# An xLSTM cell, attention and a mixture of experts on one core: x1 read in place, the experts' stages a slot further apart, the last stage in the experts' program

## The reference, cut to what matters

```
x  (32, 256, 128)                                  # B, T, D
# part 1: a gated recurrence over T, in every one of the 128 channels
pre = layernorm(x) @ W + b ;  i, f, o, z = split(pre)
m_t = max(f_t + m, i_t);  c = f_s*c + i_s*tanh(z);  n = f_s*n + i_s;  h = sig(o)*c/(n+eps)
x1 = x + h / rms(h) * scale
# part 2: on layernorm(x1)
q, k, v = split(layernorm(x1) @ w_qkv)             # 16 heads of 8
o = softmax(causal(q k^T / sqrt(8))) v @ w_o
h = layernorm(layernorm(x1) + o, g1, b1)
probs = softmax(h @ wg); the two best of 8 experts, weights normalised
moe = sum over the two of  w_e * (gelu(h @ w1_e + bb1_e) @ w2_e + bb2_e)
out = x1 + layernorm(h + moe, g2, b2)
```

## Time and profile before

| | us |
|---|---|
| median of 3 runs | 1063.59 (1061.05 to 1064.22) |
| the profiled execution | 1061.42 |
| its span, first to last instruction | 1059.6 |
| PE / DVE / ACT / POOL busy | 902.4 / 849.5 / 769.8 / 535.0 |

### The profile page before, as it was taken

How to read it: one execution, slowest core, us unless ns; L and a number is a source line. 1 busy time by engine, 2 the same in 40 slices (tenths; PEclk the granted TensorE clock), 3 DMA queues, 4 the chain that set the end, 5 groups by cost and what they waited for, 6 DMA issues and landing times. The chain is left out here.

```text
span 1059.6 us, 26142 instructions
## 1 busy us (share of the span) xinstructions
PE 902.4 (85%) x6922; PEld 698.3 (66%) x6922; DVE 849.5 (80%) x2533; ACT 769.8 (73%) x1905; POOL 535.0 (50%) x781
## 2 busy tenths in 40 slices
PE   1446899999999999999999998846999999999474
PEld 0234667676766766766676666536999999999421
DVE  4667989999999999998989888673777777777378
ACT  2776799999999999997897766751656656666356
POOL 8000243344356556656577767782555656656400
PEclk9657999999999999998999999965999999999788
DMA  1015543444354454545344556153333332332186
GB/s 52 1 51 130 132 108 108 113 118 111 90 136 118 120 128 118 136 108 124 104 127 126 137 140 160 40 119 102 88 99 86 92 89 85 95 86 67 48 247 190
DMA packets 138118, 114.69 MB, mean 108 GB/s; under 512 B 19459, under 2 KB 126601, under 8 KB 138005
## 3 DMA queue, kind: packets, MB, share of 16 engines
q1 hardware_dynamic: 120916, 92.24, 33.9%
q0 software_dynamic: 8640, 16.93, 5.0%
q10 hardware_dynamic: 8448, 4.20, 1.4%
HBM read 60.60 MB, written 52.58 MB: 107 GB/s over the span
## 5 line engine op out<-in xcount | busy, mean ns | idle before, releaser
L621 POOL TENSOR_SCALAR_AFFINE_SELECT b_PT<-b_PT 128x256 f32<-128x256 f32 (+1 forms) x384 | 191.0, 512 | 207.2 <-ACT b_PT L811 202.1
L1180 DVE TENSOR_REDUCE b_m_neg<-b_ps_m 128x2 f32<-128x512 f32 (+1 forms) x384 | 255.1, 681 | 33.9 <-PE b_ps_m L1615 15.8
L811 ACT ACTIVATE b_PT<-b_ps_s 128x512 f32<-128x512 f32 x384 | 219.6, 598 | 28.3 <-PE b_ps_s L1591 13.9
L1923 POOL DMA_INDIRECT results<-e_Y,e_X x142 | 151.7, 1068 | 121.4 <-DVE e_Y L1991 98.5
L656 POOL DMA_INDIRECT slots<-c_pay,b_pos x128 | 130.3, 1018 | 39.9 <-issue 36.5
L2039 PE MATMUL e_ps_d<-e_h,e_w 128*128 128x256 f32 x568 | 134.5, 380 | 0.0
L1615 PE MATMUL b_ps_m<-c_QK 128*128 128x256 f32 x512 | 123.3, 322 | 0.0
L1594 PE MATMUL b_ps_s<-c_QK 128*128 128x512 f32 x256 | 111.0, 434 | 5.6 <-ACT b_PT L811 5.4
L1950 ACT ACTIVATE e_h<-e_ps,e_w 128x256 f32<-128x256 f32 x284 | 111.3, 480 | 0.8 <-PE e_ps L2030 0.8
L2039 PEld LDWEIGHTS e_ps_d<-e_h,e_w 128*128 128x128 f32 x568 | 102.6, 191 | 11.0
L1943 ACT ACTIVATE e_yt<-e_ps_d,e_w 128x256 f32<-128x256 f32 x71 | 33.7, 475 | 99.2 <-PE e_ps_d L2039 99.2
(11 more groups left out here) (253 smaller groups left out, 2311.6 us busy)
## 6 DMA issues: line engine op xcount, KB each, us to landing
c_QK<-qk_scr SPq DMA_DIRECT2D x128, 192.0 KB
qk_scr<-b_qk_hi SPq DMA_DIRECT2D x64, 256.0 KB
e_X<-slots SPq DMA_DIRECT2D x71, 130.0 KB, 2.3
qk_scr<-b_qk_lo SPq DMA_DIRECT2D x32, 256.0 KB
f_G<-results SPq DMA_DIRECT2D x32, 256.0 KB, 3.6
a_X<-in_L_attn_x_dram SPq DMA_DIRECT2D x16, 256.0 KB, 6.4
x<-a_X SPq DMA_DIRECT2D x16, 256.0 KB, 2.8
b_X<-x SPq DMA_DIRECT2D x32, 128.0 KB, 5.7
```

The lines of the kernel that those rows point to most:

```text
L621: nc.gpsimd.affine_select(out=tri, in_=tri, compare_op=ALU.is_ge, fill=0.0, base=0, pattern=[[0, tri.shape[1]], [1, P]], channel_multiplie ...
L811: nc.scalar.activation(PT[:, g % 2, q % 3], ps_s[:, q % 2], ACT.Exp, scale=HD ** -0.5).then_inc(s_e, 1)
L1180: nc.vector.tensor_reduce(out, scores, AX.X, ALU.max, negate=True).then_inc(s_red, 1)
L1923: nc.gpsimd.indirect_dma_start(dram["results"][:, :], bass.IndirectOffsetOnAxis(X[:, j.of(NB_X), u, D:D + 1].bitcast(u32), 0), Y[:, n, u, ...
```

## The change

1. **x1 in place.** Attention reads x1 where GpSimd's addition leaves it (`cell_row`: a slice of `cell.X`); the buffers `X`, their loads (L518) and semaphores go. `rows_stats` waits for GpSimd's addition instead of a DMA. `cell.X` has four buffers in place of three, and a group may be loaded only when the group four before it has been normalised for attention, too. SyncE's load of a group keeps its group number per step (g = s/2 + 3 in even steps s) but moves from the first place in SyncE's step to the last, behind the four reads. Group 3 is loaded at the start.
2. **No row of zeros.** The maxima's row is partition 127, and the matmuls for the maxima read partitions 0 to 119 only; the store of zeros (L541) goes.
3. **Experts a slot further apart.** TensorE's step s has: first layer of s, rows in of s+2, rows out of s-2, second layer of s-1. The first layer's four outputs of a slot share two banks, so two slots have room; the GELUs of an output pair wait for both; `w2` has four buffers.
4. **One program.** The last stage is written behind the experts' in the same block; SyncE waits for the scatters' semaphores.
5. **Results in one piece.** Row of `results`: `(p t k) d`; a group is one DMA of 4 KB per partition.
6. **g2 by GpSimd**, VectorE keeps the addition of x1.

```diff
-NC = 3
-NX = 3
+NC = 4
-M_ROW = ROWS
+KEYS = 32 * (NJ - 1) + ROWS
+M_ROW = 127
...
+            def recurrent_in(s):
+                g = s.base // 2 - 1 + NC
+                if s.base % 2 or not NC <= g < GROUPS:
+                    return
+                stored(sync, g - NC)
+                need(sync, s_xn, Count(2 * (g - NC) + 2))
+                cell_rows(g)
...
+            def operands(b):
+                n = b.of(NQ)
+                need(sync, s_qkw[n], b.turn(NQ) * WRITES + WRITES)
+                need(sync, s_s, (b - NQ) * 12 + 12)
...
+                for j in range(NJ):
+                    sync.dma_start(QK[32 * j:32 * j + ROWS, n, j:NJ + 1:NJ - j]..., rows[j]).then_inc(s_qkr[n], 16)
             def step(s):
-                if s.base % 2 == 0 and NC <= s.base // 2 + NC < GROUPS:
-                    stored(sync, s.base // 2)
-                    cell_rows(s.base // 2 + NC)
-                if s.exists(B):
-                    sync.dma_start(X[:, n], x1_t[bass.ds(b.value(), 1)]...).then_inc(s_x[n], 16)
...
+                a, b1, x = s - 1, s - 3, group(s, 4)
+                maxima_row(b1)
+                columns_high(a)
+                columns_low(a)
+                recurrent_out(x)
+                operands(a)
+                recurrent_in(s)
...
             def rows_stats(n):
-                need(dve, s_x[k], n.turn(NX) * 16 + 16)
+                need(dve, c_x1, Count(n.base // 2 + 1))
...
# experts, TensorE
-                if (s + 1).exists(SLOTS):
-                    rows_in(s + 1)
-                if (s - 1).exists(SLOTS):
-                    rows_out(s - 1)
-                if s.exists(SLOTS):
-                    need(pe, s_yt, s)
+                if (s + 2).exists(SLOTS):
+                    rows_in(s + 2)
+                if (s - 2).exists(SLOTS):
+                    rows_out(s - 2)
+                j = s - 1
+                if j.exists(SLOTS):
+                    need(pe, s_yt, j)
...
# last stage
-    r_t = dram["results"].rearrange("(k t p) d -> p k t d", p=P, k=TOPK)
+    r_t = dram["results"].rearrange("(p t k) d -> p t k d", p=P, k=TOPK)
...
+    def on_sync(sync):
+        for sem_of, count in landed:
+            sync.wait_ge(sem_of, count)
...
+            sync.dma_start(G[:, n], r_t[:, 4 * g:4 * g + 4]).then_inc(s_g[n], 16)
...
+    def on_gpsimd(pool):
+        for g in range(GROUPS):
+            pool.wait_ge(s_y0, 4 * g + 4)
+            if g >= 2:
+                pool.wait_ge(s_y3, g - 1)
+            nc.gpsimd.tensor_tensor(Y1[:, m], Y0[:, m], kept["g_b"][:, :, :].to_broadcast([P, 4, D]), ALU.mult).then_inc(s_y1, 1)
```

More of the change, by code:

```diff
@@ L149, in cell_memory @@
         cell.r_rms = sb("a_r_rms", [P, 4])
+        cell.X = sb("a_X", [P, NC, 4, D])
     return cell
@@ L455, in cell_rooted, with cell_row @@
             return rooted(2 * g.base - 5)
+        def cell_row(b, t):
+            return cell.X[:, b.base // 2 % NC, 2 * (b.base % 2) + t, :]
         def stored(engine, g):
@@ new lines, in columns_high, with columns_low @@
+            def columns_high(b):
+                if not b.exists(B):
+                    return
+                n = b.of(NQ)
+                need(sync, s_qkhi, b + 1)
+                need(sync, s_qkr[n], b.turn(NQ) * READS)
+                slots = scr[n].rearrange("s p n -> p s n")
+                sync.dma_start(slots[:, 0:4:3], qk_hi[:, :, :].bitcast(fp32)).then_inc(s_qkw[n], 16)
+                sync.dma_start(slots[:, 1:6:4], qk_hi[:, :, :].bitcast(fp32)).then_inc(s_qkw[n], 16)
+            def columns_low(b):
+                if not b.exists(B):
+                    return
+                n = b.of(NQ)
+                need(sync, s_qklo, b + 1)
+                need(sync, s_qkr[n], b.turn(NQ) * READS)
+                slots = scr[n].rearrange("s p n -> p s n")
+                sync.dma_start(slots[:, 2:5:2], qk_lo[:, :, :].bitcast(fp32)).then_inc(s_qkw[n], 16)
@@ new lines, in recurrent_out @@
+            def recurrent_out(g):
+                if not g.exists(GROUPS):
+                    return
+                need(sync, c_x1, g + 1)
+                sync.dma_start(out_t[:, 4 * g.base:4 * g.base + 4, :], cell.X[:, g.of(NC)]).then_inc(c_out[g.of(NC)], 16)
+            def operands(b):
+                if not b.exists(B):
+                    return
+                n = b.of(NQ)
+                need(sync, s_qkw[n], b.turn(NQ) * WRITES + WRITES)
+                need(sync, s_s, (b - NQ) * 12 + 12)
+                if b.base < NQ:
+                    sync.wait_ge(s_fill, FILLED - 2 * (NQ - 1 - n))
+                rows = scr[n].rearrange("(a s) (r j g) n -> j (s r) a (g n)", a=2, g=NG, j=NJ)
+                for j in range(NJ):
+                    sync.dma_start(QK[32 * j:32 * j + ROWS, n, j:NJ + 1:NJ - j].rearrange("p a g n -> p a (g n)").bitcast(fp32), rows[j]).then_inc(s_qkr[n], 16)
@@ L1607, in maximum @@
                     for j in range(4):
-                        done = nc.tensor.matmul(ps_m[:, u % 2, j * P:(j + 1) * P], QK[:, n, j, u, 0:P], QK[:, n, NJ, u, 0:P],
+                        done = nc.tensor.matmul(ps_m[:, u % 2, j * P:(j + 1) * P], QK[0:KEYS, n, j, u, 0:P], QK[0:KEYS, n, NJ, u, 0:P],
                                                 start=False, stop=(j == 3), skip_group_check=True)
@@ L1938, in step @@
             def step(s):
-                j = s - 1
+                j = s - 2
+                if s.i is None and s.base == 0:
+                    halves(s)
+                    halves(s + 1)
                 if j.exists(SLOTS):
@@ L1996, in step @@
                     nc.vector.tensor_tensor(row, row, kept["b_b"][:, :, :], ALU.add).then_inc(s_xb, 1)
-            steps(dve, SLOTS, 1, NB_X, step, 8)
+            steps(dve, SLOTS, 2, NB_X, step, 8)
             dve.wait_ge(s_xb, NTILE)
+            last_stage["vector"](dve)
         @block.tensor
@@ L2037, in step @@
+                j = s - 1
+                if j.exists(SLOTS):
+                    need(pe, s_yt, j)
                     for c in range(NF):
-                        need(pe, s_g, s * NF + (c + 1))
-                        last = nc.tensor.matmul(ps_d[:, 0:SUB * P], w2[:, n, c * D:(c + 1) * D], h1[:, n, c], start=(c == 0), stop=(c == NF - 1))
+                        need(pe, s_g, j * NF + (c + 1))
+                        last = nc.tensor.matmul(ps_d[:, 0:SUB * P], w2[:, j.of(NB_W), c * D:(c + 1) * D], h1[:, j.of(2), c], start=(c == 0), stop=(c == NF - 1))
@@ L2179, in constants @@
+            steps(pe, SLOTS, 2, NB_X, step, 8)
+            last_stage["tensor"](pe)
 def constants(nc, ctx, dram):
```

337 lines of the change are left out of this document (152 added, 185 removed).

## The result

The changed kernel takes 1118.7 us in the median of four runs (1115.3 to 1121.5), against 1062.3 for the kernel before (1059.2 to 1064.2, four runs): a ratio of 1.053, with a 95% interval from 1.049 to 1.057. The forecast was 1128, from 1078 to 1172. The profiled execution took 1115.3 us, its span is 1113.5; that of before took 1061.4.

A forecast was written before the change was run, and what follows sets the result against it. TensorE and VectorE were taken to bound stage 1, TensorE the experts, a loop through TensorE, VectorE and ScalarE the last stage. From 1061.4 us, -12 + 52 + 26 + 1 - 2 + 1.7 = +67 gave 1128, range 1078 to 1172.

The forecast's parts named there:

- The stall: Stage 1: the group's load behind the four reads lands after 5.7 us, making VectorE 5.8 us late, twelve times.
- How much remains: Stage 1: of VectorE's lateness 4.3 us per group remains, 52 us over twelve groups; bounds 32 to 77.
- The clock: Stage 1: the granted clock falls after each TensorE standstill, costing 2.2 us on each of 12 pairs, 26 us.
- The gain of x1 in place: Stage 1: with both loads and the zeros gone from ahead of the QK reads, 12 of 13.8 us waiting saved.
- Experts: Experts' stage: the 71 slots keep their pace; the second slot's rows add +1 us at the start.
- seam: Between last scatter and last stage: one program's end and the next's start go, -2 us, between -1 and -3.
- last stage: Last stage: g2 on GpSimd costs +1 us, and +0.7 at the very end where the multiply is bare.
- The first: Rival, stage 1: the load is there in time, VectorE's idle time hides it, clock stays; 1046 us, chance 0.08.
- The second: Rival, stage 1: the stall is partly absorbed to 2.9 us per pair, no slow clock; 1085 us, chance 0.17.
- The third: Rival, stage 1: everything adds, 6.0 us per pair and 4.2 for the clock; 1178 us, chance 0.12.
- The fourth: Rival, results: rows 64 KB apart are read or scattered badly, +33 to +66 us; 1161 at half, chance 0.05.

The follow-up runs named there:

- e6: The changed kernel with 14 unused matmuls filling TensorE's standstill ahead of maxima tile 8 in the twelve odd steps; 1110.9 us, 1.045 of the kernel before.
- e1: The changed kernel with SyncE's load of a group issued right behind the maxima's row, ahead of the four reads; 1051.7 us, 0.989 of the kernel before.
- e5: Changed kernel's stage 1 with the load issued early, experts and last stage as in the kernel before; 1054.5 us, 0.992 of the kernel before.
- e10: The changed kernel with the load issued early and the experts' stages one slot apart as before, still one program; 1051.3 us, 0.989 of the kernel before.
- e3: The changed kernel with the load behind the wait for the batch's last score but ahead of the four reads; 1055.1 us, 0.993 of the kernel before.
- e7: The kernel before with only the results' rows in one piece, one DMA per group; 1064.0 us in one run.

## Why the prediction was right, point by point

- **The stall.** Forecast: the load is issued as VectorE wants it, lands 5.7 us later, VectorE is 5.8 us late, twelve times. Measured: landing 6.1 us in the median, waits of 5.6 us on average (3.9 to 7.6), twelve. The step from the earlier trace rows, that the batch's last score and the statistics hang together, held in every pair.
- **How much remains.** Forecast 4.3 us per group, from the two waits in the earlier trace rows that would vanish; TensorE's standstill at tile 8 was to be 3.8 us and was 3.8 in the median. Measured: 64.7 less 6.7 for the clock, 58.0 us, 4.8 per group against 4.3. The term was 6 us too small, and what was mis-sized in it is the absorption: 1.5 us of each 5.8 were to be hidden, but with the clock kept up (e6) 68.4 us of waiting cost 58.0, 0.9 hidden per group, and in the changed kernel 66.9 cost 64.7, 0.2 per group. VectorE's idle time is hardly a reserve for a long stall, as most of it recurs behind the stall.
- **The clock.** That it would fall in the pairs was right: 0.50 behind the standstill shown, and 0.94 in the mean over eleven pairs. The term was mis-sized: 26 us forecast, 6.7 measured; the pairs were to be 43 to 46 us long and were 42.05 in the mean. The step that failed took the 2.2 us from a pair in which TensorE led over to one in which it follows. Without this error the sum would have been 9 us below the medians' +56.4, not 11 above.
- **The gain of x1 in place.** Forecast 12, measured 9.3 between the traces of before and e1, and 11.2 between the means of the kernels with equal stage 1 (6.9 to 15.0 between single ones). Of the 13.8 us of waits for QK 12 were to go; in e1 5.2 us are left, in e5 with the same stage 1 2.7. In the changed kernel they are gone (0.2 us), probably since the stall of the odd step holds up TensorE instead.
- **Experts** +1 forecast, all of it at the start; +1.8 measured, made of 2.7 at the start and 0.9 given back (see e10); **seam** -2 forecast, -3.7 measured, beyond my bound of -3: the load of the first results starts 2.3 us behind the last scatter in place of 5.5, where I had put 3.8 for the scatter's writing and landing, and the first sum 4.1 us behind that in place of 4.6; **last stage** +1.7 forecast, +0.4 measured.
- **The sum.** +67 forecast, made of 66 for stage 1 and 1 for the rest; +53.9 by the traces, 55.4 and -1.5. That the total came within 10 us of the median is in part luck: the stall's term was 6 us too small and the clock's 19 too large, so two errors met with opposite signs. The mechanism, a late load behind the reads with everything on VectorE's list behind it, was right.
- **Rivals.** The first (in time, faster, 1046) is what e1 shows for another place of the same line: 1051.7. The second (absorbed, clock stays) failed on both points, and e3 shows where it would have held: waits of 0.3 to 2.9 us. The third (everything adds, 1178) put 6.0 us for the stall and 4.2 for the clock on each group, where 4.8 and 0.6 were found. The fourth is out by e7.

## What to carry to other kernels

When buffers are reused at closer range, the load's place in its queue moves with them: write down for each moved DMA which waits now stand ahead of it in the queue, and what is queued behind its reader. Here one line's place was worth 65 us, against the 11 to 13 that all other parts together gave, and either end mends it (load earlier: all of it; reader later: all but 9 us). Price a stall by who is late behind it: here waits of 1 or 2 us were at least partly hidden, waits of 5.6 us cost nearly their full length, and the slow TensorE clock cost much only where the others waited for TensorE.

## What the runs showed of the hardware

A load of 256 KB issued right behind four reads of 192 KB landed in 6.1 us in the median (changed kernel), and in 3.1 us with none ahead of it (e3); both from the same queue. The granted clock fell to 0.50 behind a standstill of 4.04 us that followed full work. It was 0.94 in the mean over eleven such pairs, and 0.99 with 14 matmuls of 0.24 us in that place, though these computed nothing that was used. Kernels with the same code in stage 1 ended it up to 4.8 us apart from one run to another, more than several of the changes here are worth.
